# Graph attention on one core: GpSimd holds the gathers of a group until all rows of the group before have landed

## The reference, cut to what matters

```python
def gat_conv(x, src, dst, edge_attr, W, att_src, att_dst, W_e, att_e, bias, n_nodes):
    xp = (x @ W).reshape(-1, Hh, C)                    # 8 heads of 32
    alpha = a_src[src] + a_dst[dst] + a_edge
    alpha = leaky_relu(alpha, 0.2)
    m = segment_max(alpha, dst); ex = exp(alpha - m[dst])
    alpha = ex / (segment_sum(ex, dst)[dst] + 1e-16)
    msg = xp[src] * alpha[:, :, None]
    return segment_sum(msg, dst).reshape(n_nodes, Hh * C) + bias
xn = layernorm(x)
x = x + gnn(xn)  + mix(xn)      # gnn: two gat_conv layers; mix: an attention without softmax
x = x + ffn(layernorm(x))       # six experts, the best two of each row
```

## Time and profile before

| what | us |
|---|---|
| timed runs | 3548.32, 3561.06, 3565.73; median 3561.06 |
| the profiled execution | 3566.32 |
| its span, first to last instruction | 3564.4 |
| busy: PE, DVE, ACT, POOL | 2549.3, 2146.7, 1130.1, 2046.6 |
| first to last message, layer 0 and layer 1 | 177.6 to 1488.5, 1650.7 to 2969.0 |

### The profile page before, as it was taken

One profiled execution on the slowest core, in us unless ns is written; L12 is line 12 of the kernel. 1 busy time (PEld: TensorE's weight loads), 2 busy tenths in 40 slices (PEclk: granted clock), 3 DMA queues, 4 the chain that ended last, 5 costly groups with the idle time before them and its releaser, 6 DMA issues. The chain is left out here.

```text
span 3564.4 us, 57920 instructions
## 1 busy us (share of the span) xinstructions
PE 2549.3 (72%) x15613; PEld 2149.2 (60%) x15614; DVE 2146.7 (60%) x6378; ACT 1130.1 (32%) x3915; POOL 2046.6 (57%) x2269
## 2 busy tenths in 40 slices
PE   5376876777777777764777676767676766859897
PEld 4265655655666565644666666656566664648786
DVE  6265666666666665634666665656666666676565
ACT  3133333333333333441222222222222223532222
POOL 3465665565656565365565565656566553636665
PEclk9677777777777777786677776777777767969999
DMA  9544544444444444134444444544444442554443
GB/s 238 168 136 124 139 127 131 132 130 132 133 134 134 132 134 133 50 113 121 136 138 138 137 139 127 146 127 141 134 141 136 138 124 74 166 146 153 141 120 93
DMA packets 282383, 475.56 MB, mean 133 GB/s; under 512 B 69124, under 2 KB 191644, under 8 KB 282116
## 3 DMA queue, kind: packets, MB, share of 16 engines
q0 software_dynamic: 96912, 288.68, 29.9%
q1 hardware_dynamic: 120884, 137.12, 12.5%
q10 hardware_dynamic: 64320, 46.56, 4.2%
HBM read 398.47 MB, written 75.78 MB: 133 GB/s over the span
## 5 line engine op out<-in xcount | busy, mean ns | idle before, releaser
L708 POOL DMA_INDIRECT e_rows<-table,e_idx x1664 | 1610.0, 968 | 1091.9 <-DVE e_msg L749 665.1
L1094 PE MATMUL e_ps_sum<-e_hot,e_msg 128*128 128x128 f32 x6656 | 1196.5, 339 | 251.4 <-DVE e_msg L749 139.4
L1094 PEld LDWEIGHTS e_ps_sum<-e_hot,e_msg 128*128 128x128 f32 x6656 | 1058.0, 242 | 309.0 <-DVE e_msg L749 173.8
L946 ACT ACTIVATE acc<-e_ps_sum 128x256 f32 x1664 | 641.8, 386 | 1574.3 <-remote 929.3
L749 DVE TENSOR_TENSOR e_msg<-e_rows,e_ps_pr 128x256 f32<-128x256 f32 x1664 | 672.2, 416 | 40.3 <-PE e_ps_pr L1085 11.3
L1074 PE MATMUL e_ps_al<-e_dst_score,e_hotT 128*128 x3328 | 331.3, 186 | 376.5 <-issue 209.9
L1074 PEld LDWEIGHTS e_ps_al<-e_dst_score,e_hotT 128*128 128x128 bf16 x3328 | 258.0, 104 | 522.4 <-issue 452.5
L738 DVE TENSOR_SCALAR e_hotT<-e_relb,pcolf 128x512 bf16<-128x512 bf16 x416 | 147.6, 355 | 495.5 <-remote 380.6
L724 DVE TENSOR_TENSOR e_hot<-e_ps_pr,rel 128x508 f32<-128x508 f32 x416 | 283.5, 682 | 0.0
L767 DVE TENSOR_TENSOR e_al<-e_ps_al,e_rows 128x128 f32<-128x128 f32 x104 | 30.3, 292 | 381.5 <-remote 201.4
L2292 ACT ACTIVATE x_h<-x,eb 128x128 f32<-128x128 f32 x216 | 67.9, 366 | 277.9 <-PE x L2366 229.7
(11 more groups left out here) (370 smaller groups left out, 3562.8 us busy)
## 6 DMA issues: line engine op xcount, KB each, us to landing
e_relb<-rel_rows SPq DMA_DIRECT2D x104, 512.0 KB
e_rows<-table,e_idx POOLq DMA_INDIRECT x1664
e_eattr<-in_edge_b SPq DMA_DIRECT2D x104, 128.0 KB
e_xT<-turned_x ACTq DMA_DIRECT2D x100, 128.0 KB
e_xr<-in_x ACTq DMA_DIRECT2D x100, 128.0 KB
node<-l_row SPq DMA_DIRECT2D x25, 512.0 KB, 3.2
table<-t_row SPq DMA_DIRECT2D x25, 276.0 KB
table<-j_row SPq DMA_DIRECT2D x25, 276.0 KB, 2.5
```

The costliest lines, as they stand in the source:

```text
L708: nc.gpsimd.indirect_dma_start(out=rows[q][:, k, :], out_offset=None, in_=table[0:NP], in_offset=bass.IndirectOffsetOnAxis(ap=idx[:, q, k: ...
L946: nc.scalar.activation(acc[:, :, bass.ds(at[k + e], P)], ps_sum[pair % 3][:, e], ACT.Copy).then_inc(s["window"], 1)
L1094: op = nc.tensor.matmul(ps_sum[pair % 3][:, e, a], msg[:, (16 * g + k + e) % RM, a * P:a * P + P], hot[:, (4 * g + k // 4) % RH, (k + e) % ...
```

## The change

POOL gets one more wait, before the first gather of each group but the first: all 16 gathers of the preceding group must have landed. No instruction is moved, added or taken away on any other engine.

```diff
@@ -702,6 +702,8 @@
             def gather(g, q):
 
                 pool.wait_ge(s["idx"], g + 1)
+                if g > 0:
+                    pool.wait_ge(s[f"rows{1 - q}"], 256 * ((g - 1) // 2) + 256)
                 for k in range(GT):
 
                     pool.wait_ge(s["msg"], 16 * g + k + 1)
```

## The result

| | us |
|---|---|
| changed kernel, 4 timed runs | 3688.19 to 3696.23, median 3693.55 |
| kernel before, 4 timed runs | 3548.32 to 3565.73, median 3558.88 |
| ratio, 95% interval | 1.0379, 1.035 to 1.0408 |
| profiled execution of the changed kernel | 3688.19, span 3686.3 |

The change costs 3.8%, 135 us. The prediction said 3650 us, slower, within 3530 to 3775. All lines behind the edit are 2 further down than before. PE, DVE, ACT and POOL are TensorE, VectorE, ScalarE and GpSimd.

A forecast was written before the change was run, and what follows sets the result against it. It took the loop of DVE and PE as the bound, PE's signals being late during unbroken gathers. 3566.3 + 107 (pauses) - 16 (starts) = 3657, 5 lower for timed runs, 3652, rounded to 3650 us; range 3530 to 3775.

The forecast's parts named there:

- The added wait itself costs nothing: POOL ahead of gather 0: delay of 1.7 to 2.2 us, covered by pauses of 1.78 and 2.93 us; direct cost nothing.
- The shape of the pauses: Steady groups: pause moves ahead of gather 0, the one before gather 5 goes; 1.05 us a group, 107 us.
- The bounds, 0 and 2.1: Cost per group: 0 if the pauses' shape meant nothing, 2.1 us (214 us in all) if every group became like the example.
- the example: Group of the kernel before where DVE was late, gathers 0 to 7 without a pause; took 27.4 us against 25.3 on average.
- the choice of the middle: Steady groups: 1.05 us taken, since the scores' signal for L767 may come sooner, giving back up to 1.9 us.
- another line: Sign in DVE's waits: more before L778, L738 or another line that waits for PE or for ACT behind PE.
- The starts, -16 us: Layer starts: a pause amid the 32 gathers lets L767 start sooner; 8 us saved in each layer, ends 0 and -44.
- my reading: While POOL sends gathers without a pause, PE's signals reach others late, in a burst once POOL stood still 1 to 4 us.
- The signs to look for: Gather 0 3.2 to 3.7 us after gather 15, no pause between gathers 4 and 5, L767's wait below 381.5 us, groups near 26.4.
- Nothing changes: Rival: the wait lies in POOL's idle time and the late signals have their own cause in PE; 3561 us, chance 0.20.
- Faster: Rival: L767 starts 1.9 us sooner, nothing held later, if transpose L1081 gets through; 3448 us, chance 0.17.
- Landing on the path: Rival: pauses too short, gather 15 and the next group's rows late; 173 us more, 3734 us, chance 0.06.

The follow-up runs named there:

- e5_longer_pause: Kernel before, with a POOL instruction of about 2.94 us ahead of gather 0 of every group but the first, no wait for landing: 1.0449, 3745 us.
- e2: Kernel before, with the added wait in group 1 of each layer alone (2 waits instead of 102): 0.9945, 3540 us.
- e3: Kernel before, with the added wait in every group but 1 (100 of the 102 waits): 1.045, 3716 us.
- e1: Kernel before, with a POOL instruction of some 2.3 us ahead of gather 0 of every group but the first, no wait for landing: 1.0201, 3629 us.
- e6: The changed kernel, plus a POOL instruction of about 1.7 us ahead of gather 5 of every group: 1.0054 to the kernel before, 3602 us.
- e12: Kernel before, with a POOL instruction of about 1.7 us ahead of gather 5 of every group, e9 repeated in another series: 0.9856, 3532 us.
- e8: Kernel before, with gathers fetching only the first 128 columns of each row, the other columns zeroed at each layer's start: 1.000.
- e9: Kernel before, with a POOL instruction of about 1.7 us ahead of gather 5 of every group, no wait for landing: 1.0608, 3177 us (kernel before 2997).
- e4: Kernel before, with a short POOL memset ahead of every gather: 0.9922, 3534 us.

## Why the prediction was right

*The added wait itself costs nothing* held as far as the landing goes: e5_longer_pause costs as much without waiting for one. The pauses that hide it weren't worthless, though. The prediction said so in its next step, and that step carries the whole loss.

*The shape of the pauses, 1.05 us a group, 107 us:* right in sign and cause, too small. Measured are 160.0 / 102 = 1.57 us. The bounds, 0 and 2.1, held, but the upper one stood on a wrong footing: 25.3 us came from dividing the stretches by 52, while 27.4 was measured from gather 15 to gather 15. That distance is 25.8 us on average in the kernel before (groups 3 to 49 of both layers). So the example was 1.6 us longer than the average and not 2.1, and 102 x 1.6 = 163 us is nearly what was measured. The example was also one group: the 32 groups of the kernel before with no more than 1 us of pause ahead of gather 5 take 26.8 us on average. That 107 us came as near as it did is partly luck.

The part that failed is the choice of the middle, because DVE isn't late at the group's beginning and L767 could give back up to 1.9 us. It gave back 119 us in all, 381.5 less 262.4, or 1.2 us a group; but the transpose took 130 us again and the wait for ACT 94 us, which the list of signs had only as "another line". I had counted the first wait that the new pause frees and only halfway the next ones that fall into the longer row of gathers 0 to 7.

*The starts, -16 us:* right in sign, between its ends of 0 and -44, with 20 to 25 us measured (e2, e3). In layer 0 L769 didn't wait at all (22.45 us before), but 9.21 us of it came back before L740; the prediction had allowed for waits there:

```profile
139.15 0.28 DVE L769 TENSOR_TENSOR e_al<-e_ps_al,e_rows 128x128 f32<-128x128 f32 x1
...
148.24 0.35 DVE L740 TENSOR_SCALAR e_hotT<-e_relb,pcolf 128x512 bf16<-128x512 bf16 x1 [1.62 <-PE e_ps_al L1076]
...
158.07 0.35 DVE L740 TENSOR_SCALAR e_hotT<-e_relb,pcolf 128x512 bf16<-128x512 bf16 x1 [9.21 <-remote]
```

These rows also correct *my reading*, that the signals come in a burst when POOL has stood still for 1 to 4 us. POOL sends its second 16 gathers in one row, from 139.78 to 159.50. PE's scores for the first L740 reach DVE 8.5 us into that row, and the second L740, whose scores PE had ended by 150.42 (L1076), goes on at 158.07, 1.4 us before the row ends. Some signals pass during a row, and a late one need not wait for its end. What is shown is that the place of POOL's pauses decides how long DVE waits, not which signal is held and until when.

*The signs to look for:* gather 0 comes 3.78 us after gather 15 in the group above, above the 3.2 to 3.7 foretold for nearly all groups; only 39 of the 94 groups counted lie within, the other 55 above. There is no pause between gathers 4 and 5, L769's wait below 381.5, the transpose's above. From gather 15 to gather 15 that group takes 1038.97 - 1012.26 = 26.7 us; the mean over both layers is 27.5, where I had put 26.4 (and 25.8 is the mean before).

*The rivals.* "Nothing changes", with the rule of the Trainium skill (SBUF — State Buffer, "Who interferes with whom": DMA never contends with a compute engine) beside it: e1, e5, e6 and e12 differ from the kernel before in POOL's list alone, and the ratio goes from 0.986 to 1.045. The rule itself isn't contradicted, since halving the gathers' bytes changed nothing (e8); it just doesn't reach this effect. "Faster": L767 came sooner as it said, but its condition, that the transpose still gets through, failed: in the group above it came 4.2 us after gather 0 and was late. "Landing on the path": its 173 us are near the 160 of the groups by chance only, since no landing is needed for them.

*What stays open.* Whether it is PE's signal or PE's instruction that is held: PE's waits for "issue" ahead of L1094 rose too, from 111.0 to 261.4 us. ACT is late too, so the cause need not lie in DVE; but no run changed what PE, DVE or ACT do. What makes the series of e9 different: the kernel of e9 was granted a clock of 0.834 there and of 0.779 in e12, and no run tells whether this is a cause or a result. And the change was not run there.

## What to carry to other kernels

An engine's idle time is not free to move. Before a wait is put into it, look at what the other engines do in the moments when it stands still: here DVE often went on just then. Where gathers go out in a long row and the waits for TensorE end together after it, try a short deliberate pause at the place where the waited-for result is ready, and judge a wait by the sum over all waits behind it, not by the one it frees. Repeat such a test in more than one series and on more than one chip: here the same pause gained 1.4% in one series and lost 6% in another.

## What the runs showed of the hardware

- In three of the four series and in the traces of the prediction and the change, DVE went on late after a matmul's recorded end while GpSimd sent indirect gathers 1.25 us apart: 5.5 us late in the group above (1020.49 to 1026.02, 3.31 us of it idle), 22.6 us at the start of layer 0 (144.23 to 166.87). In the ordinary groups shown it went on 0.3 us (above) or 1.7 us (1023.05 to 1024.76) after the row's end.
- Not every signal is late in a row, and a late one does not always wait for its end: the scores of 1018.50 reached DVE in 0.04 us, a signal passed at 148.24, 8.5 us into a row, and DVE was released at 158.07, 1.4 us before that row's end.
- A GpSimd instruction of 1.7 us in the row shortens the wait (e6: 200.5 to 40.0 us for the transpose), so the engine need not be idle, only not sending gathers. A memset of 0.22 us between every two gathers does little (e4: 360.6 and 190.2 us of unnamed waits instead of 380.6 and 201.4).
- It doesn't depend on the gathers' bytes (162.58 or 288.68 MB in the queue, ratio 1.000).
- In the series of e9 it didn't show (28.2 us of waiting for the one-hot tiles' products and 1.3 us for the transpose; 583.6 and 8.3 us in e12 with the same kernel), and the kernel before took 2997 us instead of 3561 to 3587. How much of that difference is due to it, these runs don't tell.
- A memset of 223 ns before each gather widens the distance between gathers by 0.09 us only: most of it fits into the 0.30 us of "issue" between them.
